# A four-layer graph network on one core: kept rows of the attention stage summed in pairs, and some rows of x gathered one stage early

## The reference, cut to what matters

```
h = relu(layernorm(x));  x = x + L0(h)     # GCN: rows scaled by 1/sqrt(deg), summed over dst, @W, prelu
h = relu(layernorm(x));  x = x + L1(h)     # edge_weight * h[src], summed over dst, @W.T + b
h = relu(layernorm(x));  x = x + L2(h)     # attention, below
h = relu(layernorm(x));  x = x + L3(h)     # edge and node MLPs on h[src], h[dst], summed over dst

# L2, with one more edge from every node to itself ("loop")
e     = exp(leaky_relu(a_src[src] + a_dst[dst]) - m[dst])
alpha = e / (segment_sum(e, dst) + 1e-16)
out   = segment_sum(h[src] * alpha, dst) + gat_bias
mean, var = out.mean(axis=0), out.var(axis=0)          # over all nodes
out   = relu(gamma * (out - mean) * rsqrt(var + eps) + beta + h)
```

## Time and profile before

| | us |
|---|---|
| median of 3 runs | 2882.89 (2882.42 to 2883.62) |
| the profiled execution | 2887.68 |
| its span in the trace | 2886.2 |
| histogram stage, POOL's first gather to the next stage's first load | 31.4 to 127.4 |
| first layer's stage, POOL's first to its last gather | 128.2 to 886.6 |
| attention stage, first product to last norm column | 1593.9 to 1837.7 |

### The profile page before, as it was taken

The page is one execution under the profiler, slowest core; times in us unless marked ns, Lnnn a source line. Parts: engine busy times, 40 slices in busy tenths (PEclk is TensorE's granted clock), DMA queues, the critical chain, the costliest instruction groups (busy, mean ns, idle before and its releaser), DMA issues. The chain is left out here.

```text
span 2886.2 us, 53025 instructions
## 1 busy us (share of the span) xinstructions
PE 2158.4 (75%) x11615; PEld 1499.1 (52%) x11615; DVE 1877.8 (65%) x8597; ACT 1788.4 (62%) x4580; POOL 1433.2 (50%) x1442
## 2 busy tenths in 40 slices
PE   3376666666664888858885899666663999999996
PEld 1154444444443677747785566433332666666663
DVE  8786767676674777758886455477775555555552
ACT  0097777777774788859994233499994444444442
POOL 5277777777774666537771000000002466666663
PEclk9898888898987999979996899899996999999998
DMA  1155555555553566646662443299997222223320
GB/s 37 40 176 159 167 159 172 154 175 154 176 157 106 141 170 172 166 132 186 198 201 62 130 114 109 68 302 307 303 308 209 64 72 72 78 81 81 78 74 24
DMA packets 443512, 413.60 MB, mean 143 GB/s; under 512 B 54123, under 2 KB 339902, under 8 KB 443338
## 3 DMA queue, kind: packets, MB, share of 16 engines
q1 hardware_dynamic: 379146, 337.34, 38.5%
q0 software_dynamic: 64192, 74.09, 10.1%
HBM read 233.85 MB, written 181.23 MB: 144 GB/s over the span
## 5 line engine op out<-in xcount | busy, mean ns | idle before, releaser
L1979 POOL DMA_INDIRECT x_bx<-t_X,k_bslot x2 | 2.0, 1016 | 646.6 <-DMA t_X<-k_S 646.2
L2238 POOL DMA_INDIRECT out_dram<-mlp_ou,mlp_iro x200 | 200.2, 1001 | 186.4 <-issue 185.8
L474 POOL DMA_INDIRECT second_xs<-t_X,second_irs x200 | 200.1, 1000 | 128.9 <-issue 50.8
L474 POOL DMA_INDIRECT first_rd<-t_R,a_irs x200 | 200.7, 1004 | 108.7 <-issue 60.3
L474 POOL DMA_INDIRECT a_xd<-in_x_dram,a_ird x200 | 213.4, 1067 | 66.4 <-issue 59.7
L2231 POOL DMA_INDIRECT mlp_xs<-t_X,mlp_irs x200 | 202.1, 1010 | 77.7 <-issue 59.7
L474 POOL DMA_INDIRECT a_xs<-in_x_dram,a_irs x200 | 206.4, 1032 | 60.9 <-issue 60.6
L474 POOL DMA_INDIRECT project_xs<-t_X,project_irs x200 | 200.7, 1003 | 63.8 <-issue 59.8
L2291 DVE TENSOR_TENSOR mlp_v<-mlp_ps_r,mlp_b 126x512 f32<-126x512 f32 x50 | 34.6, 692 | 238.7 <-ACT mlp_y L2350 235.4
L2393 PE MATMUL mlp_ps_e<-mlp_h,mlp_we 128*128 128x504 f32 x400 | 188.2, 594 | 1.2 <-ACT mlp_h L2372 1.2
L2405 PE MATMUL mlp_ps_m<-mlp_e,mlp_wn 128*128 128x504 f32 x400 | 185.3, 586 | 0.0
(11 more groups left out here) (394 smaller groups left out, 7127.5 us busy)
## 6 DMA issues: line engine op xcount, KB each, us to landing
t_X<-first_x SPq DMA_DIRECT2D x194, 256.0 KB, 3.3
first_x<-in_x_dram SPq DMA_DIRECT2D x97, 256.0 KB, 4.2
project_x<-t_X SPq DMA_DIRECT2D x97, 256.0 KB, 3.2
x_x<-t_X SPq DMA_DIRECT2D x97, 256.0 KB, 4.2
t_X<-x_x SPq DMA_DIRECT2D x97, 256.0 KB, 4.5
out_dram<-x_ou SPq DMA_DIRECT2D x97, 256.0 KB, 4.7
t_G<-second_g SPq DMA_DIRECT2D x50, 267.8 KB
t_X<-first_xo SPq DMA_DIRECT2D x50, 252.0 KB
```

The source lines that it names most:

```text
L474: pool.indirect_dma_start(dst[:, q, :], None, table, bass.IndirectOffsetOnAxis(ap=idx[:, q:q + 1], axis=0)).then_inc(s_rows, 16)
L2238: pool.indirect_dma_start(out, bass.IndirectOffsetOnAxis(ap=iro[s][:, q:q + 1], axis=0), OU[s][:, q, :], None, bounds_check=N - 1, oob_is_ ...
```

## The change

1. In the histogram stage POOL gathers groups 0 to 2 ahead, not 0 to 3. Then it gathers the destination rows of x for the NX = 12 groups 4, 8, ..., 48 into 12 buffers `D` of their own. SP stores each of these to a new DRAM table XD, ten before the two stores of R and two behind, and the stage ends when they are stored.
2. In the first layer's stage POOL no longer gathers `Xd` for t >= 4 with t % 4 == 0; it gathers `Xs` and `Xd` of group 3 there instead. SP loads `Xd[0]` from XD in one DMA, behind the dense loads and a wait for `e_x1`. VectorE waits for it beside the gathers.
3. In the attention stage the products are masked: `rec` is multiplied by `lastc` before the products (one more VectorE instruction and a wait). VectorE then adds the four tiles of rows and of squares in pairs, into `SM` (two more instructions of 256 elements per partition). The eight norm matmuls of a group become two of 256 columns, with ones as weights.
4. On TensorE the two L1846 of a group move: each stands behind tile 1 and tile 3 of the group before. The norm matmuls stand behind tiles 0 and 2, and belong to the group four behind. `M` and `U` have four buffers instead of two, and VectorE weighs group t+1 after the products of group t-2.

```diff
+        self.s_own = m.ring("own_gathered", NX)
...
-        for g in range(4):
+        for g in range(3):
             gate(kp, pool, kp.s_first_idx, g + 1)
             gather_rows(pool, kp.Xs[g], a["x"], kp.irs[g], kp.s_gathered[g])
             gather_rows(pool, kp.Xd[g], a["x"], kp.ird[g], kp.s_gathered[g])
+        for j in range(NX):
+            gather_rows(pool, D[j], a["x"], kp.dsti[:, 4 * (j + 1) * GT:(4 * (j + 1) + 1) * GT], s_dg[j])
...
+        def keep(j):
+            sp.wait_ge(s_dg[j], 16 * GT)
+            sp.dma_start(slot_rows(T["XD"], j), D[j][:, :, :]).then_inc(s_ds, 16)
+
+        for j in range(NX - 2):
+            keep(j)
         sp.wait_ge(s_d, 19)
...
+        for j in range(NX - 2, NX):
+            keep(j)
         sp.wait_ge(s_st, 32)
+        sp.wait_ge(s_ds, 16 * NX)
...
+            if u == 0 and there(t, NGE) and not before(t, 4):
+                gate(kp, sp, e_x1, t - 3)
+                sp.dma_start(Xd[0][:, :, :], T["XD"].rearrange("(k p) d -> p k d", p=RW)[:, bass.ds(t - 4, GT), :]).then_inc(s_own, 16)
...
             if not before(t, 4):
                 gate(kp, pool, e_m, (t - 3) * GT)
+            if not before(t, 3):
                 gather_rows(pool, Xs[u], a["x"], irs[u], s_rows[u])
+            if u and not before(t, 4):
                 gate(kp, pool, e_x1, t - 3)
+            if u and not before(t, 3):
                 gather_rows(pool, Xd[u], a["x"], ird[u], s_rows[u])
...
+                dve.tensor_tensor(rec[:, :, :], rec[:, :, :],
+                                  kp.lastc[:, bass.ds(g * GT, GT)].unsqueeze(2).to_broadcast([RW, GT, H]), ALU.mult).then_inc(s_mk, 1)
+                dve.wait_ge(s_mk, g + 1)
...
+            weigh(t + 1, (u + 1) % 4)
+            g, s = t - 4, u
+            if there(g, NGE):
+                dve.wait_ge(s_sq, g + 1)
+                if not before(g, 2):
+                    dve.wait_ge(s_n, g - 1)
+                dve.tensor_tensor(SM[s % 2][:, :, 0, :], kp.rows(g)[:, 0:2, :], kp.rows(g)[:, 2:4, :], ALU.add)
+                dve.tensor_tensor(SM[s % 2][:, :, 1, :], OQ[s][:, 0:2, :], OQ[s][:, 2:4, :], ALU.add).then_inc(s_ad, 1)
...
-                pe.matmul(psN[0:1, 0:128], kp.lastc[:, k:k + 1], kp.rows(g)[:, q, :], start=k == 0, stop=k == NT - 1)
-                ins = pe.matmul(psN[0:1, 512:640], kp.lastc[:, k:k + 1], OQ[s][:, q, :], start=k == 0, stop=k == NT - 1)
...
+            if b == 0:
+                pe.wait_ge(s_ad, g + 1)
+            ins = pe.matmul(psN[0:1, 0:256], kp.ones[0:RW, 0:1], SM[s % 2][:, b, :, :].rearrange("p w d -> p (w d)"), start=g == 0 and b == 0, stop=g == NGE - 1 and b == 1)
...
+                if q % 2 == 0:
+                    norms(gn, sn, q // 2)
+                else:
+                    own(t, u, q // 2)
```

More of the change, by code:

```diff
@@ L39 @@
 NGE = NT // GT
+NX = (NGE - 1) // 4
 SLOTS = NT * RW
@@ L507, in phase_hist @@
                                                   sem("root"), sem("rtable_stored"))
+    D = [sb(f"d{j}", [RW, GT, 128]) for j in range(NX)]
+    s_dg, s_ds = kp.s_own, sem("own_stored")
     block = m.ctx.enter_context(nc.Block())
@@ L760, in stats @@
                         dve.bn_stats(st[r][0:p, XD * h + q, :], X[2 * u + h][0:p, q, :])
-            dve.wait_ge(s_rows[u], landed(t, u, 4, 3 * GT) + gathered[u])
+            dve.wait_ge(s_rows[u], complete(t, u) + gathered[u])
+            if u == 0 and not before(t, 4):
+                dve.wait_ge(s_own, landed(t - 4, 0, 4))
             for w, x in enumerate((Xs[u], Xd[u])):
@@ L1711, in phase_attend @@
     Gd = [sb(f"gd{i}", [RW, GT, 128]) for i in range(4)]
-    M = [sb(f"m{i}", [RW, GT, MW]) for i in range(2)]
-    U = [sb(f"u{i}", [RW, GT, MW]) for i in range(2)]
+    M = [sb(f"m{i}", [RW, GT, MW]) for i in range(4)]
+    U = [sb(f"u{i}", [RW, GT, MW]) for i in range(4)]
     den = sb("den", [RW, GT, H])
@@ L1716, in phase_attend @@
     OQ = [sb(f"oq{i}", [RW, GT, 128]) for i in range(4)]
+    SM = [sb(f"sm{i}", [RW, 2, 2, 128]) for i in range(2)]
     row = sb("row", [1, 256])
     psO = [m.ps(f"o{i}", [128, 1024]) for i in range(2)]
-    psN = m.ps("norm", [128, 1024])
+    psN = m.ps("norm", [128, 512])
     psC = m.ps("norm_columns", [128, 512])
```

88 lines of the change are left out of this document (46 added, 42 removed).

## The result

The changed kernel takes 2803.57 us (median of 4 runs, 2803.09 to 2805.97), the kernel before takes 2883.26 beside it (2882.42 to 2885.25). The ratio is 0.9724, with a 95% interval of 0.9707 to 0.9741: 79.7 us or 2.8% faster. The forecast was 2813, with 2795 to 2838 as the range. The profiled execution took 2805.97 us, against 2887.68 before: 81.7 less.

The account below looks back on a forecast made before the run. POOL's issue was taken to bound the first layer, VectorE the histogram, PE the attention stage. 58.5 - 18.5 = 40 us plus 30 us make 70 less: 2887.7 to 2817.7 profiled, 2813 as median, range 2795 to 2838.

Parts of the forecast that it names:

- What bounds each stage: POOL's issue sets the first layer (1.328 us a gather), VectorE the histogram loop, PE's serial products and identity products the attention.
- The first layer: First layer's stage: POOL issues 528 gathers instead of 568, first to last gather 699.9 us, 58.5 us less.
- rival (c): First layer: the load from XD reaches VectorE late, staged groups still take 15.9 us; 7 less in all, 2876; chance 0.06.
- The histogram's end: Histogram stage: 72 gathers instead of 32, last start at 137.1, next stage's first load at 145.9, 18.5 us later.
- The attention stage: Attention stage: the group's period falls from 4.69 to 4.10 us over 46.6 groups; with start and end 30 us less.
- the step to the fourth: Attention stage on PE: third product at 3.15 us, fourth at 4.10, counted from the previous group's fourth product.
- the stage's start: Attention stage: the first three groups, at the lower clock, give about 1 us.
- rival (b): Attention stage: VectorE becomes the bound, period 4.4 us; 55 less in all, 2828; chance 0.17.
- rival (a): Attention stage: the carry alone sets the pace, period 3.80 us; 84 less in all, 2799; chance 0.14.
- rival (d): Attention stage: TensorE loses its full clock, 6.4 us a group; slower, 2923; chance 0.05.
- histogram step: Histogram stage: gathers start every 1.575 us while VectorE's loop runs, then every 1.33; VectorE's pace hardly changes beside them.

Follow-up runs that it names:

- own_rows_last: The changed kernel with group 2's own eight gathers moved behind the staged ones in the histogram stage: 2806.81 us, ratio 0.9721.
- no_pair_sums: The changed kernel without VectorE's two pair sums; the norm matmuls read tiles 0 and 1 directly: 2803.57 us, ratio 0.9722.

## Why the prediction was right

**What bounds each stage** held. The first layer's step is 700.56 / 527 = 1.329 us, forecast 1.328; VectorE's wait for landing fell to 2.8 us a group, forecast 3, and did not go. (The prediction's 4.5 a group before is 4.5 a wait; a group it was 4.1.)

**The first layer** gave 57.9 us, forecast 58.5, and the load from XD cost nothing, so rival (c) falls. Not in the sum were 3.0 us behind the last gather. VectorE starts the last group 2.61 us after that gather's start (845.91 to 848.52) instead of 4.16, and from there to the second layer it is 22.4 us instead of 23.8; no row before told either.

**The histogram's end** moved by 17.2 us, forecast 18.5. The steps were right: 1.575 us until the loop ended, then 1.34 on average (I took 1.33), and the last start at 137.37, forecast 137.1. From there I had 8.7 us to the first load, by the data's landing and the store. It was 7.2, and `own_rows_last` shows that neither is what it waits for. That this term came out near is luck.

**The attention stage** gave 36.5 us, forecast 30. This is the term that was too small. The period is 4.01 us, not 4.10: 46.6 groups x 0.09 = 4.2 us more. `den` to products took 0.94 us (0.63 + 0.30 = 0.93 forecast), and the identity product waits 0.33 us, as forecast. Counted from a fourth product (1623.64), the identity product that waits starts at 2.67 (1626.31), forecast 2.65, and the third product 0.52 later (1622.28 to 1622.80), at 3.19, forecast 3.15. Two misses cancel in the 2.67: `den` starts at 0.83 instead of 0.91, and from the products' end to the identity product it is 0.15 instead of 0.05. What was too long is the step to the fourth: 0.84 (1622.80 to 1623.64), where I had 0.95. Behind a wait the carry catches up a little. The rest is the stage's start: from the first identity product to the first squares it takes 10.7 us instead of 14.5, 3.8 less where I put 1. About 2 us of that are luck of this execution. The granted clock rose from 0.50 to 1.00 at 4.1 us behind the first identity product (it is 0.90 on average from 1550 to 1555), before the change at 14.7. In `own_rows_last`, with the same attention code, it rose at 12.5, the start took 12.9 us and the stage 209.7 instead of 207.7. So the period is the mis-sized term, and the stage's start was nearly right.

**The chain, not VectorE, sets the new period.** `no_pair_sums` refutes rival (b), and the runs with the mask in the divisor show what rival (a) would have been: a mean period of 3.80 us, as I had it, and 9 us less in the stage than the changed kernel, where I had 14. After the stage's start the clock kept 1.00, so rival (d) falls, although PE is idle 8% of the time. The Trainium skill, page "TensorE: Matmul & The Clock Gate", section "HAM oscillation — how this bites in real kernels", warns that waits between groups of matmuls can throttle the engine again. With 0.3 us each, once a group, the rows here don't show it.

**On other chips the forecast would have been wrong.** Its histogram step took from the rows that VectorE's pace hardly changes beside gathers. On the two slower chips it falls to a seventh some 20 us into the gathers, and the staged half turns from 44 us gained into 54 and 59 lost. The change as a whole was not run there; with the mask in the divisor it is level with the kernel before (0.9989 and 0.9993), and the mask is worth about 10 us.

## What to carry to other kernels

Where one engine's issue sets a stage, move its work into a stage where it idles, and cost the move by that stage's own step; but look first whether the stage's other engines keep their pace beside it, on more than one chip. Where a chain with a carry sets the pace, a small instruction between the carry and what frees the buffer counts until the next chain takes over: 0.33 us of mask cost 0.2 us a group, and then the carry's own 3.80 us set the pace. The 0.75 us of extra work beside the chain cost nothing. Where a step of a sum fits in size, its reason may still be another. And where a stage starts at the lower clock, one execution's start says little; look at several.

## What the runs showed of the hardware that was not expected

- A stage ended 7.2 us after POOL's last indirect DMA started, with POOL idle for 6.99 us, no matter whether a store of its data followed and although no DMA engine had moved anything for more than 4 us.
- Beside a VectorE loop with a step of 0.394 us gathers started every 1.575 us, with one of 0.678 every 1.355: four times and twice the loop's step. The first seven gathers of the stage kept 1.38 on average.
- On the two slower chips VectorE, in the histogram's loop, kept its pace beside POOL's gathers for some 20 us, then executed one instruction every 1.40 us until about 8 us after the last gather, and one every 0.197 us afterwards. Where the kernel before takes 2883 us instead of 3430.7, the gathers didn't slow it.
- The attention stage begins at the lower clock, and with the changed code the granted clock rose 4.1 us after the stage's first product in one execution and 12.5 us after it in another; the stage took 207.7 and 209.7 us.
